# First attention's loop in double steps, second attention's normalisation moved to the end of the key passes

## Chip, cores and metric

The kernel runs on one core of a Trainium2 chip. The metric is the device time of one execution in microseconds (us), as a median over runs: 3865.53 us before the change (3 runs, 3864.57 to 3865.61). A difference of 0.2% is 7.7 us.

## What is computed

Two layers, each an attention, a state-space scan and a feed-forward part, every one added to x. The change touches only the two attentions:

```python
# first attention: one batch entry at a time, 16 entries, 64 queries each, context of 1601 keys
q = (query @ Wq).reshape(b, sq, NUM_HEADS, HEAD_DIM).transpose(0, 2, 1, 3)     # 32 heads of 16
k = (key @ Wk).reshape(b, sk, NUM_KV_HEADS, HEAD_DIM).transpose(0, 2, 1, 3)    # 8 key heads
v = (value @ Wv).reshape(b, sk, NUM_KV_HEADS, HEAD_DIM).transpose(0, 2, 1, 3)
scores = jnp.einsum('bhqd,bhkd->bhqk', q, k) * scale
probs = jax.nn.softmax(scores, axis=-1)
out = jnp.einsum('bhqk,bhkd->bhqd', probs, v) ... @ Wo
# second attention: the same with 16 heads of 96, 4 key heads, over context and latents
```

x has 16 entries of 64 tokens and 512 channels; all is float32.

## The kernel before, in words

Every engine has its own program, written out by hand in the order in which it runs; semaphores tie them together. An instruction that waits holds up all that stands behind it on its engine.

**First attention** (`l0_attention`, the tiles named A_...). A first block makes the queries of all entries and the keys and values of entry 0. Then `all_batches` runs over the 16 entries j, which are called batches. A batch has 26 steps: the 4 key heads of half g = 0 over 13 key tiles k of 128 (the last has 65), then those of g = 1. What TensorE (PE) does in a step:

- `scores` (L1053): 4 matmuls into psE, by the keys Kst and queries Qst, in two row groups of 50 rows at once. psE is held once: the step's exponential on ScalarE (ACT, L1020, into one of 3 tiles probs) must have read it before the next step's scores.
- `maximum` (L754): one unit of the row maxima of the *next* half: a matmul pair into psX, which holds two units. VectorE (DVE) reduces each (L724). A half has 16 units: 0 to 3 over the first 512 keys, 4 to 7 and 8 to 11 over 384 each, 12 to 15 over 321. After the last, three small DVE operations and `max_rows` (L763) turn the maxima into rows, which DVE copies into Qst (L735).
- `weigh` (L1068) of the step *before*: 8 matmul instructions in four column groups (17 columns wide), probs by values, into psO.
- `project` (L785): a third or half of a chunk of the next batch's keys (K, in g = 0) or values (V, in g = 1): 12 passes for each of 4 chunks of 512, 384, 384 and 321 columns, over the full array, into psY. After a V chunk's two steps a third ("T", L774) turns it over with transposes through psY, and ACT copies it out into V (L716, `drain`).

So a step has up to three kinds of PE work, and each kind uses the array in another shape: row groups of 50 (scores, maxima), column groups of 17 (weigh), the full array (project, turns, max_rows).

```python
for u in units[:1]:
    maximum(pe, *to, u)
scores(n)
for u in units[1:]:
    maximum(pe, *to, u)
if n:
    weigh(n - 1)
key, passes = projection(s // 2, s % 2, k)
```

A K chunk goes: PE passes, ACT copy to Kf, GpSimd (POOL) split into high and low parts (L698, L699), then SyncE (SP) writes it to DRAM (L672), waits until that has landed, and reads it back in four pieces in the layout of Kst (L678); the maxima of the next batch's first half are the first to need it. SP does the four chunks one after the other (`stack_k`), and between them saves sums and reciprocals (`save`) and, after the second, loads a chunk of context (`reload`, L664). After the 13 tiles of a half ACT copies psO out (`sums_out`, L1007), and DVE takes one reciprocal of it (L1032, 256 columns), in front of unit 4 of a half.

**Second attention** (`l1_attention`, tiles named D_...): again 16 batches; between the scores and weighing of one batch and the next, PE makes the next batch's keys (L1802, K chunk c, third t), values (L1812) and maxima (L1840) through two psY buffers. DVE copies each third out in two operations, high part (L1756) and low part (L1757), reduces the maxima (L1762), and in `normalise` takes the reciprocal of the denominators (L2149) and multiplies the sums with it (L2152).

Of the kernel before, what the change touches and what calls it, by code (L numbers as in the profile page):

```python
# [12 lines left out]
P = 128  # L13
# [520 lines left out]
def l0_attention(nc, consts, X, x_rows, ctx_in, Wq, Wk, Wv, k_scratch, q_scratch, o_scratch, den_scratch):  # L534
# [17 lines left out]
    NX = NU + 1  # L552
# [4 lines left out]
    K_STEPS = [(0, 3), (3, 3), (6, 3), (9, 3)]  # L557
    PASSES = [(c, a, a2) for c in range(DC) for a, a2 in ((0, 0), (0, 1), (1, 0))]

    def maxima(k):  # L560

        return range(min(NU, NU * k // 10), min(NU, NU * (k + 1) // 10))

    def projection(j, g, k):

        for c in range(NC if j + 1 < B else 0):
            if g == 0:
                first, count = K_STEPS[c]
                if first <= k < first + count:
                    n = len(PASSES) // count  # L570
                    return ("K", j + 1, c), range(n * (k - first), n * (k - first) + n)
            elif k // 3 == c:
                if k % 3 == 2:
                    return ("T", j + 1, c), None
                n = len(PASSES) // 2
                return ("V", j + 1, c), range(n * (k % 3), n * (k % 3) + n)
        return None, None

    with ExitStack() as stack:
# [54 lines left out]
        def step_body(first):  # L634
# [6 lines left out]
            def nth_y(key):  # L641
                kind, b, c = key
                if first:
                    return c if kind == "K" else NC + 2 * c + "VT".index(kind)
                return 3 * NC * (b - 1) + (c if kind == "K" else NC + 2 * c + "VT".index(kind))

            def nth_x(b, g, u):
                return u if first else NX * (2 * b + g - 1) + u

# [68 lines left out]
            def read_maxima(dve, link, b, g, between=None):  # L718
                for u in range(NU):
                    if between and u == 4:  # L720
                        between()
                    x, w = nth_x(b, g, u), CH[u // 4][1]
                    dve.wait_ge(x_full, x + 1)
                    nc.vector.tensor_reduce(mxc[:, u % 4, :, u // 4], psX[:, x % 2, :, 0:w], axis=AX_X, op=ALU.max  # L724
                                            ).then_inc(x_free, 1)
                dve.wait_ge(x_free, nth_x(b, g, NU))
# [4 lines left out]
                x = nth_x(b, g, NU)  # L731
# [6 lines left out]

            def maximum(pe, b, g, u):
                x, c4, pair, qt = nth_x(b, g, u), u // 4, 2 * g + u % 4 // 2, u % 2  # L740
# [17 lines left out]
            def max_rows(pe, b, g):  # L758
                x = nth_x(b, g, NU)
                pe.wait_ge(x_free, x - 1)  # L760
                pe.wait_ge(mp_ready, x // NX + 1)
                for n in range(4):
                    last = nc.tensor.matmul(psX[:, x % 2, 0, bass.ts(n, P)], mpz[:, n, :], identr[:, :],  # L763
                                            start=True, stop=True)
                last.then_inc(x_full, 1)
# [35 lines left out]
            def first_batch():  # L801


                with nc.Block() as block:
# [68 lines left out]
                    def _(dve):  # L873
# [23 lines left out]
                        read_maxima(dve, link, 0, 0)  # L897
# [47 lines left out]
            def all_batches():  # L945
# [3 lines left out]
                with nc.Block() as block:  # L949
                    @block.sync  # L950
                    def _(sp):
# [7 lines left out]
                        def save_reciprocals(s):  # L959
                            sp.wait_ge(inverted, s + 1)  # L960
# [6 lines left out]
                        for j in range(B):  # L967
                            if j > 0:
                                sp.wait_ge(e_full, STEPS * j)
                            if j + 1 < B:  # L970
                                queries(sp, j + 1)
                                for c in range(NC):
# [3 lines left out]
                                    if c == 1 and j > 0:  # L976
                                        reload(sp, NC * j - 1)
# [23 lines left out]
                    def _(act):  # L1001
                        def sums_out(s):
                            act.wait_ge(probs_used, KT * (s + 1))
                            if s >= 2:
                                act.wait_ge(o_out[s % 2], 16 * (s // 2))
                                act.wait_ge(inverted, s - 1)
                            nc.scalar.activation(OT[:, s % 2, :], psO[:, 0:HQ], ACT.Copy).then_inc(o_copied, 1)  # L1007

                        for n in range(N):
                            s, k = divmod(n, KT)  # L1010
                            if k:
                                done, passes = projection(s // 2, s % 2, k - 1)
                                if done and (passes is None or passes[-1] == len(PASSES) - 1):
                                    drain(act, done)
                            if s and k == 1:
                                sums_out(s - 1)
                            if n >= NPR:
# [3 lines left out]
                                                 psE[0:KW[k], :], ACT.Exp, scale=HD ** -0.5).then_inc(e_free, 1)  # L1021
                        sums_out(2 * B - 1)

                    @block.vector
                    def _(dve):
                        link = Chain(dve, dch)

                        def invert(s):
                            dve.wait_ge(o_copied, s + 1)
                            if s >= 2:  # L1030
                                dve.wait_ge(rec_out[s % 2], 16 * (s // 2))
                            nc.vector.reciprocal(RT[:, s % 2, :], OT[:, s % 2, :]).then_inc(inverted, 1)  # L1032

                        nc.vector.memset(psO[:, 0:HQ], 1.0).then_inc(sums_cleared, 1)
                        for s in range(1, 2 * B):
                            read_maxima(dve, link, s // 2, s % 2, (lambda: invert(s - 2)) if s >= 2 else None)
                        for s in range(2 * B - 2, 2 * B):
                            invert(s)

                    @block.tensor  # L1040
                    def _(pe):
                        def scores(n):
# [4 lines left out]
                            if k == 0 and s:  # L1047
                                pe.wait_ge(x_free, nth_x(j, g, NU) + 1)
# [9 lines left out]
                        def weigh(n):  # L1058
# [5 lines left out]
                            for c, (t0, nt) in enumerate(TILES):  # L1064
                                if g == 0 and k == t0 and j:
                                    pe.wait_ge(y_free, nth_y(("T", j, c)) + 1)
# [9 lines left out]
                        for n in range(N):  # L1076
                            s, k = divmod(n, KT)
                            to = divmod(s + 1, 2)
                            units = maxima(k) if to[0] < B else ()
                            for u in units[:1]:  # L1080
# [1898 lines left out]
```

## Time and profile before

| | |
|---|---|
| median of 3 runs | 3865.53 us |
| the profiled execution's own time | 3856.49 us |
| its span | 3854.8 us |
| PE busy | 3619.2 us, 94% |
| DVE busy | 2254.2 us, 58% |
| ACT busy | 1607.5 us, 42% |
| POOL busy | 1281.2 us, 33% |
| first attention's scores, first to last start | 102.6 to 1009.6 us |
| second attention's keys, first to last start | 1397.3 to 3043.4 us |

The terms below are taken against the span of the profiled execution, of which its own time is 1.7 us more; the median is 9.0 us above that time, so a difference found in the span is subtracted from the median. A busy PE is not a PE at its peak, since a matmul's recorded length contains its way through the array: what work costs is read from start to start.

### The profile page before, as it was taken

What the parts mean: (1) busy time and instruction counts of PE and PEld (TensorE: products, weight loads), DVE (VectorE), ACT (ScalarE), POOL (GpSimd) and SP (SyncE); (2) the same over time, 40 slices, a digit from 0 to 9 for tenths busy, and PEclk for the clock granted to TensorE, in tenths of its full rate; (3) what the DMA queues carried; (4) which work ended last, traced back from release to release, by engine and by line L of the source; (5) the groups of instructions that cost most, each with busy time, mean ns of one, the idle gap of its engine ahead of it and who ended that gap; (6) DMA issues with size and microseconds to landing.
All of it is one profiled execution on the core that took longest, in us unless ns stands there. A gap on an engine that the chain in (4) does not pass through costs nothing. (4 is left out here: it accounts for less than half of the span.)

```text
span 3854.8 us, 75904 instructions
## 1 busy us (share of the span) xinstructions
PE 3619.2 (94%) x32856; PEld 2526.8 (66%) x32856; DVE 2254.2 (58%) x2469; ACT 1607.5 (42%) x2213; POOL 1281.2 (33%) x792
## 2 busy tenths in 40 slices
PE   7999999999779779999999999999999998797998
PEld 4555556555345555788888888888888846454554
DVE  4666666666369852555555555555555515697972
ACT  2555555555269421222222222222222103697950
POOL 4344344342048520222222222222221004285861
PEclk8999999999789889999999999999999999898999
DMA  6455555553111032111111111111111112111110
GB/s 209 126 136 148 141 140 147 141 138 103 41 55 52 12 142 80 29 42 41 49 41 49 41 41 50 41 49 41 49 41 45 72 42 55 41 51 31 52 45 22
DMA packets 215252, 277.14 MB, mean 72 GB/s; under 512 B 67056, under 2 KB 165328, under 8 KB 213632
## 3 DMA queue, kind: packets, MB, share of 16 engines
q1 hardware_dynamic: 214920, 272.28, 24.3%
q8 instruction: 261, 4.28, 0.5%
q14 instruction: 71, 0.58, 0.1%
HBM read 218.63 MB, written 53.13 MB: 70 GB/s over the span
## 5 line engine op out<-in xcount | busy, mean ns | idle before, releaser
L1727 POOL TENSOR_TENSOR D_ctx_lo<-D_ctx_raw,D_ctx_hi 128x2048 fp32r<-128x2048 f32 (+1 forms) x64 | 269.7, 4214 | 1217.8 <-ACT D_ctx_hi L1721 1217.8
L724 DVE TENSOR_REDUCE A_mxc<-A_psX 128x2 f32<-128x768 f32 (+2 forms) x512 | 485.4, 984 | 206.1 <-PE A_psX L754 205.2
L1020 ACT ACTIVATE A_probs<-A_psE 128x1024 f32<-128x1024 f32 (+1 forms) x416 | 426.3, 1025 | 317.3 <-PE A_psE L1053 312.0
L1746 ACT ACTIVATE D_V<-D_psY 128x384 f32<-128x384 f32 x208 | 101.9, 490 | 904.3 <-PE D_psY L1812 904.3
L1762 DVE TENSOR_REDUCE D_mxc<-D_psE 128x4 f32<-128x1536 f32 (+2 forms) x128 | 241.9, 1890 | 235.0 <-PE D_psE L1840 235.0
L2103 ACT ACTIVATE D_probs<-D_psE 128x2048 f32<-128x2048 f32 x112 | 210.4, 1879 | 295.6 <-PE D_psE L2216 295.6
L330 POOL TENSOR_TENSOR ES_hcp<-E_du,E_Cn 128x512 f32<-128x512 f32 x224 | 284.8, 1275 | 128.3 <-DVE E_du L357 97.9
L2232 PE MATMUL D_psO<-D_probs,D_V 128*32 128x256 f32 (+1 forms) x5376 | 313.4, 381 | 0.0
L1802 PE MATMUL D_psY<-D_ctx_hi,D_wk_hi 128*128 128x384 f32 (+2 forms) x768 | 279.9, 364 | 13.4 <-DVE D_K_lo L1757 12.7
L1812 PE MATMUL D_psY<-D_wv_hi,D_ctx_hi 128*128 128x384 f32 x832 | 285.3, 343 | 0.0
L1812 PE MATMUL D_psY<-D_wv_hi,D_ctx_lo 128*128 128x384 f32 x832 | 279.0, 335 | 0.0
L1812 PE MATMUL D_psY<-D_wv_lo,D_ctx_hi 128*128 128x384 f32 x832 | 278.5, 335 | 0.0
L357 DVE TENSOR_TENSOR_SCAN E_du<-ES_dA,ES_dB 128x512 f32<-128x512 f32 x224 | 262.4, 1205 | 19.0 <-PE ES_dB L401 12.5
L1802 PE MATMUL D_psY<-D_ctx_hi,D_wk_lo 128*128 128x384 f32 (+2 forms) x768 | 268.3, 349 | 0.0
L1802 PE MATMUL D_psY<-D_ctx_lo,D_wk_hi 128*128 128x384 f32 (+2 forms) x768 | 268.2, 349 | 0.0
L1068 PE MATMUL A_psO<-A_probs,A_V 128*17 128x256 f32 (+1 forms) x3328 | 267.7, 394 | 0.2 <-ACT A_probs L1020 0.2
L2143 DVE TENSOR_TENSOR D_acc<-D_acc,D_probs 128x1024 f32<-128x1024 f32 x96 | 135.8, 1415 | 213.7 <-ACT D_probs L2103 212.1
L2232 PEld LDWEIGHTS D_psO<-D_probs,D_V 128*32 128x32 f32 (+1 forms) x5376 | 163.2, 110 | 115.8 <-issue 9.0
L754 PE MATMUL A_psX<-A_Kst,A_Qst 50*128 50x384 f32 (+2 forms) x1024 | 217.1, 421 | 12.4 <-DVE A_mxc L724 5.9
L417 PE MATMUL ES_acc<-ES_hcp,all_ident 128*128 128x512 f32 x448 | 228.3, 596 | 0.0
L401 PEld LDWEIGHTS ES_dB<-all_ident,ES_scaled 128*128 128x128 f32 x1024 | 128.1, 145 | 133.6 <-issue 80.1
L2211 PE MATMUL D_psE<-D_Q_hi,D_K_hi 32*128 32x256 f32 (+1 forms) x2688 | 207.9, 294 | 5.7 <-PEq L49 5.7
(369 smaller groups left out, 7793.9 us busy)
## 6 DMA issues: line engine op xcount, KB each, us to landing
A_land<-in_ctx SPq DMA_DIRECT2D x32, 768.0 KB, 6.1
D_ctx_raw<-in_ctx SPq DMA_DIRECT2D x32, 768.0 KB, 4.7
A_land<-in_ctx SPq DMA_DIRECT2D x16, 1024.0 KB, 5.7
D_ctx_raw<-in_ctx SPq DMA_DIRECT2D x16, 1024.0 KB, 5.4
E_Cn<-bc_scratch SPq DMA_DIRECT2D x64, 256.0 KB, 3.3
k_scratch<-A_Khl SPq DMA_DIRECT2D x32, 384.0 KB, 5.2
A_Kst<-k_scratch SPq DMA_DIRECT2D x64, 192.0 KB, 3.6
A_land<-in_ctx SPq DMA_DIRECT2D x16, 642.0 KB, 4.4
```

Source lines behind the costliest of these rows:

```text
L330: nc.gpsimd.tensor_tensor(hcp[:, k % NP, :], h_sb[:, k % NP, :], rows.C[:, q % NR, :], ALU.mult).then_inc(hcp_ready, 1)
L357: nc.vector.tensor_tensor_scan(to, decay(s), entering, 0.0, ALU.mult, ALU.add).then_inc(h_ready, 1)
L417: nc.tensor.matmul(acc[:, c, :], consts["ident"][:, :], product, start=(n == 0), stop=(n == N_STATE - 1)).then_inc(summed, 1)
L724: nc.vector.tensor_reduce(mxc[:, u % 4, :, u // 4], psX[:, x % 2, :, 0:w], axis=AX_X, op=ALU.max).then_inc(x_free, 1)
L754: last = nc.tensor.matmul(psX[:, x % 2, o, 0:w], Qst[b % 2][rows, pair, P * qt:P * qt + P], Kst[b % 2][rows, pair, k0:k0 + w], start=True, ...
L1020: nc.scalar.activation(probs[0:KW[k], n % NPR, :, :].rearrange("p h q -> p (h q)"), psE[0:KW[k], :], ACT.Exp, scale=HD ** -0.5).then_inc(e ...
L1068: last = nc.tensor.matmul(psO[32 * h:32 * h + HD + 1, 0:HQ], V[j % 2][0:KW[k], k, HG * g + h, :], probs[0:KW[k], n % NPR, 2 * (h % 2) + h ...
L1727: nc.gpsimd.tensor_tensor(ctx_lo[c][:, :, 0:w], ctx_raw[c][:, :, 0:w], ctx_hi[c][:, :, 0:w].bitcast(F32), ALU.subtract).then_inc(lo_done[c ...
L1762: nc.vector.tensor_reduce(mxc[:, H * a:H * a + H, c], psE[:, :, 0:CH[c][1]], axis=AX_X, op=ALU.max).then_inc(x_free, 1)
L1802: last = nc.tensor.matmul(to[:, 0:w], wk_parts[a][:, d, bass.ts(t, P)], parts[a2][:, d, 0:w], start=(n == 0), stop=(n == len(PASSES) - 1))
L1812: last = nc.tensor.matmul(to[0:KWD[k], 0:H * HD], parts[a][:, d, at], wv_parts[a2][:, d, :], start=(n == 0), stop=(n == len(PASSES) - 1))
L2232: last = nc.tensor.matmul(psO[32 * h:32 * h + 32, t, :], V[0:KWD[k], k, h, bass.ts(t, 32)], probs[0:KWD[k], N % NPR, h, bass.ts(i, NQ)], s ...
```

## The change

In the first attention the 26 steps of a batch become 13 double steps d (0 to 12; `HALVES`, `RUNS`, `UNITS`, `TURNS` are tables by d). In a double step PE does: scores of the even step, up to two maxima, the weighing of the two steps *before*, scores of the odd step, the third maximum, then, all on the full array, the rows of maxima (d = 5 and 12), six or twelve passes of projection, and the turn of a V chunk (d = 8, 10, 12, and 0 of the next batch). At d = 6 the last tile of the first half is weighed by itself right after the next scores, so that d = 7 has one to weigh. The maxima of a half begin at d = 6 (first half of the next batch) and d = 12 (second half), and their rows are turned in the double step behind the last unit. A turned V chunk now goes through psX and is copied by DVE, not through psY and ACT. SP loads the context chunk after all four K chunks. The reciprocal is taken in two halves of 128 columns at d = 1, 2 and 8, 9.

In the second attention DVE's `normalise(j)` moves from behind the first maximum to behind the last K third.

```diff
+    TWOS = STEPS // 2
+    HALVES = (range(6), range(6, 12))
+    RUNS = [("K", 0, HALVES[0]), ("K", 0, HALVES[1]), ("K", 1, HALVES[0]), ("K", 1, HALVES[1]),
+            ("K", 2, range(12)), ("K", 3, range(12)), ("V", 0, HALVES[0]), ("V", 0, HALVES[1]),
+            ("V", 1, HALVES[0]), ("V", 1, HALVES[1]), ("V", 2, HALVES[0]), ("V", 2, HALVES[1]), ("V", 3, range(12))]
+    TURNS = {8: 0, 10: 1, 12: 2, 0: 3}
+    ROWS_FIRST, ROWS_BEHIND = 5, 12
+    UNITS = ((3, 3, 2, 3, 3, 2), (2, 3, 3, 3, 3, 2))
...
+            def values_out(dve, key):
+                b, c = key[1:]
+                x, (t0, nt) = nth_x(key), TILES[c]
+                dve.wait_ge(x_full, x + 1)
+                nc.vector.tensor_copy(V[b % 2][:, t0:t0 + nt, :, 0:HD],
+                                      psX[:, x % 2, 0, 0:P * nt].rearrange("p (j h d) -> p j h d", j=nt, h=H)
+                                      ).then_inc(x_free, 1)
...
                                     stack_k(sp, j + 1, c)
                                     if c == 0 and j > 0:
                                         save(2 * j - 1)
-                                    if c == 1 and j > 0:
-                                        reload(sp, NC * j - 1)
+                                if j > 0:
+                                    reload(sp, NC * j - 1)
...
+                        for j in range(B):
+                            for d in range(TWOS):
+                                exponential(STEPS * j + 2 * d)
+                                exponential(STEPS * j + 2 * d + 1)
+                                key, passes = projection(j, d)
+                                if key and passes[-1] == len(PASSES) - 1:
+                                    drain(act, key)
...
+                        weighed = 0
+                        for j in range(B):
+                            for d in range(TWOS):
+                                n = STEPS * j + 2 * d
+                                behind, ahead = maxima(j, d)
+                                scores(n)
+                                for _, b, g, u in behind:
+                                    maximum(pe, b, g, u)
+                                for e in range(weighed, n):
+                                    weigh(e)
+                                weighed = n
+                                scores(n + 1)
+                                for _, b, g, u in ahead:
+                                    maximum(pe, b, g, u)
+                                if (n + 1) % KT == 0:
+                                    weigh(n)
+                                    weighed = n + 1
+                                if rows_of(j, d):
+                                    max_rows(pe, *rows_of(j, d)[1:])
+                                key, passes = projection(j, d)
+                                if key:
+                                    project(pe, key, passes)
+                                if turned(j, d):
+                                    turn(pe, turned(j, d))
...
                     read_maxima(dve, nxt, 0)
-                    normalise(j)
                     keys_out(dve, link, nxt, 1, 0)
                     keys_out(dve, link, nxt, 1, 1)
...
                         keys_out(dve, link, nxt, c + 1, 2)
+                    normalise(j)
                     read_maxima(dve, nxt, 6)
```

PE in the first attention's loop, before: the end of a project block, one step, and the start of its project block (L785 projects, L754 is a maximum, L1053 scores, L1068 weighs).

```order
L785 MATMUL A_psY<-A_ctx_hi,A_wvlo 128x512
L754 MATMUL A_psX<-A_Kst,A_Qst 128x512 x2
L1053 MATMUL A_psE<-A_Qst,A_Kst 128x256 x4
L754 MATMUL A_psX<-A_Kst,A_Qst 128x512 x2
L1068 MATMUL A_psO<-A_probs,A_V 17x256 x4
L785 MATMUL A_psY<-A_ctx_hi,A_wvhi 128x512
L785 MATMUL A_psY<-A_ctx_lo,A_wvhi 128x512
```

PE at the same loop after the change, double step d = 0 of a batch up to its first passes (L832 projects, L790 is a maximum, L1123 scores, L1138 weighs).

```order
L1123 MATMUL A_psE<-A_Qst,A_Kst 128x256 x4
L790 MATMUL A_psX<-A_Kst,A_Qst 128x512 x4
L1138 MATMUL A_psO<-A_probs,A_V 17x256 x8
L1123 MATMUL A_psE<-A_Qst,A_Kst 128x256 x4
L790 MATMUL A_psX<-A_Kst,A_Qst 128x384 x2
L832 MATMUL A_psY<-A_ctx_hi,A_wkhi 128x512
L832 MATMUL A_psY<-A_ctx_lo,A_wkhi 128x512
```

Two steps' weighing now stands in one block, and one project block follows two scores instead of one.

DVE in the second attention around the first maximum, before (L1756 and L1757 copy a K third, L1762 reduces a maximum, L2149 and L2152 normalise).

```order
L1757 TENSOR_TENSOR D_K_lo<-D_psY,D_K_hi 128x512
L1762 TENSOR_REDUCE D_mxc<-D_psE 128x4
L2149 RECIPROCAL D_recip<-D_psO 128x256
L2152 TENSOR_TENSOR D_OT<-D_psO,D_recip 128x12x64
L1756 CAST D_K_hi<-D_psY 128x384
```

The same engine after the change, at the last K third of a batch (L1835 and L1836 copy, L2228 and L2231 normalise, L1841 reduces).

```order
L1835 CAST D_K_hi<-D_psY 128x385
L1836 TENSOR_TENSOR D_K_lo<-D_psY,D_K_hi 128x385
L2228 RECIPROCAL D_recip<-D_psO 128x256
L2231 TENSOR_TENSOR D_OT<-D_psO,D_recip 128x12x64
L1841 TENSOR_REDUCE D_mxc<-D_psE 128x4 x2
```

The two operations now stand behind all copies of K and in front of the last two maxima.

## Rows read from the trace of the kernel before

**Rows 1.** Engines by stretch, one batch: us, PE, PEld, DVE, ACT, POOL busy, PEclk, DMA, GB/s
```profile
445.00:502.00 57.00, 56.50 (x494) 33.80 (x493) 38.11 (x44) 32.99 (x41) 25.42 (x17) 1.00 0.54 143
```

**Rows 2.** Timeline of PE, first attention: first scores of two batches (start, length)
```profile
446.02 0.49 PE L754 MATMUL A_psX<-A_Kst,A_Qst 50*128 50x512 f32 x2
446.74 0.50 PE L1053 MATMUL A_psE<-A_Qst,A_Kst 50*128 50x256 f32 x4 [0.22 <-ACT A_probs L1020]
...
503.93 0.50 PE L1053 MATMUL A_psE<-A_Qst,A_Kst 50*128 50x256 f32 x4 [0.21 <-ACT A_probs L1020]
```

**Rows 3.** Timeline of PE, one step and the blocks around it
```profile
448.29 0.39 PE L785 MATMUL A_psY<-A_ctx_hi,A_wklo 128*128 128x512 f32 x1
448.52 0.39 PE L785 MATMUL A_psY<-A_ctx_hi,A_wkhi 128*128 128x512 f32 x1
448.84 0.49 PE L754 MATMUL A_psX<-A_Kst,A_Qst 50*128 50x512 f32 x2
449.17 0.39 PE L1053 MATMUL A_psE<-A_Qst,A_Kst 50*128 50x256 f32 x4
449.40 0.39 PE L754 MATMUL A_psX<-A_Kst,A_Qst 50*128 50x512 f32 x2
449.72 0.63 PE L1068 MATMUL A_psO<-A_probs,A_V 128*17 128x256 f32 x8
450.28 0.50 PE L785 MATMUL A_psY<-A_ctx_lo,A_wkhi 128*128 128x512 f32 x1
450.61 0.40 PE L785 MATMUL A_psY<-A_ctx_hi,A_wklo 128*128 128x512 f32 x1
```

**Rows 4.** Timeline of PE, second attention: a weighing of six steps' size in one block
```profile
1900.00 2.80 PE L2232 MATMUL D_psO<-D_probs,D_V 128*32 128x256 f32 x48
1902.62 0.62 PE L2242 MATMUL D_psO<-D_acc,D_ones 128*32 128x256 f32 x8
```

**Rows 5.** Timeline of PE, last batch: two scores with only the exponential between
```profile
980.96 0.50 PE L1053 MATMUL A_psE<-A_Qst,A_Kst 50*128 50x256 f32 x4 [0.48 <-ACT A_probs L1020]
...
982.64 0.50 PE L1053 MATMUL A_psE<-A_Qst,A_Kst 50*128 50x256 f32 x4 [0.62 <-ACT A_probs L1020]
```

**Rows 6.** Timelines of PE and SP: chunk K0 from its last pass to its write
```profile
453.44 0.39 PE L785 MATMUL A_psY<-A_ctx_hi,A_wklo 128*128 128x512 f32 x1
...
456.53 0.38 SPq L672 DMA_DIRECT2D k_scratch<-A_Khl  x1
```

**Rows 7.** Timeline of SP: chunk K2 written and read back, K3 written; landing times of these transfers
```profile
472.14 0.56 SPq L672 DMA_DIRECT2D k_scratch<-A_Khl  x1
478.70 2.46 SPq L678 DMA_DIRECT2D A_Kst<-k_scratch  x4
481.29 0.50 SPq L672 DMA_DIRECT2D k_scratch<-A_Khl  x1
...
DMA to landing us min/median/max: 2.8/3.7/7.4
```

**Rows 8.** Last batch: engines by stretch (columns of rows 1), and timeline of PE in it
```profile
993.00:1000.00 7.00, 6.24 (x44) 2.48 (x40) 0.00 (x0) 3.56 (x4) 0.00 (x0) 0.50 0.00 0
...
993.54 0.80 PE L1053 MATMUL A_psE<-A_Qst,A_Kst 50*128 50x256 f32 x4 [0.19 <-ACT A_probs L1020]
994.27 1.06 PE L1068 MATMUL A_psO<-A_probs,A_V 128*17 128x256 f32 x8
...
995.52 0.80 PE L1053 MATMUL A_psE<-A_Qst,A_Kst 50*128 50x256 f32 x4 [0.19 <-ACT A_probs L1020]
```

**Rows 9.** Timelines of DVE and PE, second attention's key passes
```profile
1839.16 1.76 DVE L1762 TENSOR_REDUCE D_mxc<-D_psE 128x4 f32<-128x1540 f32 x1 [5.84 <-PE D_psE L1840]
...
1906.39 1.75 DVE L2149 RECIPROCAL D_recip<-D_psO 128x256 f32<-128x256 f32 x1
...
1909.05 0.55 DVE L1756 CAST D_K_hi<-D_psY 128x384 fp32r<-128x384 f32 x1
...
1910.24 0.44 PE L1802 MATMUL D_psY<-D_ctx_hi,D_wk_hi 128*128 128x384 f32 x1 [0.85 <-DVE D_K_lo L1757]
```

More of the change, by code:

```diff
@@ new lines, in turned, with rows_of, maxima @@
+    def turned(j, d):
+        b = j if d == 0 else j + 1
+        return ("T", b, TURNS[d]) if d in TURNS and 1 <= b < B else None
+    def rows_of(j, d):
+        if d == ROWS_FIRST:
+            return ("R", j, 1)
+        return ("R", j + 1, 0) if d == ROWS_BEHIND and j + 1 < B else None
+    def maxima(j, d):
+        if d < ROWS_FIRST:
+            b, g, at = j, 1, d + 1
+        elif d < ROWS_BEHIND:
+            b, g, at = j + 1, 0, d - ROWS_FIRST - 1
+        else:
+            b, g, at = j + 1, 1, 0
+        if j == 0 and d < ROWS_FIRST:
+            us = range(NU * d // ROWS_FIRST, NU * (d + 1) // ROWS_FIRST)
+        else:
+            us = range(sum(UNITS[g][:at]), sum(UNITS[g][:at + 1]))
+        units = [("M", b, g, u) for u in us] if b < B else []
+        return units[:2], units[2:]
@@ L579, in l0_attention @@
+    TURN_OF_X = []
+    for j in range(B):
+        for d in range(TWOS):
+            behind, ahead = maxima(j, d)
+            TURN_OF_X += behind + ahead + [key for key in (rows_of(j, d), turned(j, d)) if key]
+    place_x = {key: n for n, key in enumerate(TURN_OF_X)}
     with ExitStack() as stack:
@@ L764, in max_rows, with turn @@
                                             start=True, stop=True)
+                last.then_inc(x_full, 1)
+            def turn(pe, key):
+                b, c4 = key[1:]
+                x = nth_x(key)
+                pe.wait_ge(y_free, nth_y(("V", b, c4)) + 1)
+                pe.wait_ge(x_free, x - 1)
+                for t in range(TILES[c4][1]):
+                    last = nc.tensor.transpose(psX[:, x % 2, 0, bass.ts(t, P)], VT[:, c4 % 2, bass.ts(t, P)],
+                                               consts["ident"][:, :])
                 last.then_inc(x_full, 1)
@@ L1005, in sums_out, with exponential @@
                                 act.wait_ge(o_out[s % 2], 16 * (s // 2))
[L1006 removed]
+                                act.wait_ge(inverted, 2 * s - 2)
                             nc.scalar.activation(OT[:, s % 2, :], psO[:, 0:HQ], ACT.Copy).then_inc(o_copied, 1)
[L1009 removed]
+                        def exponential(n):
                             s, k = divmod(n, KT)
[L1011 to L1014, printed above, removed]
                             if s and k == 1:
```

118 lines of the change are left out of this document (56 added, 62 removed).

## The prediction

> **What bounds the kernel now.** I read the engines by stretch first. In a batch of the first attention PE is busy 56.5 of 57 us at a granted clock of 1.00 (2.4 GHz), DVE 38.1, ACT 33.0, POOL 25.4 [rows 1]: PE sets the end, and the others have room. Then the timeline of PE. The first scores of two batches stand 57.19 us apart (446.74, 503.93) [rows 2]; fifteen batches run like this, the sixteenth has nothing to project. In it PE hardly waits, so the question is what its time is made of, and that is read from start to start inside a step [rows 3]. A projecting pass of 512 columns takes 0.23 us when another follows (448.29 to 448.52), 0.32 when a maximum follows (448.52 to 448.84), and 0.33 as first of its block (450.28 to 450.61). A maximum of 512 columns takes 0.33 behind a pass and 0.32 in front of a weighing, while scores between two maxima take 0.23. So a block on the full array costs 0.19 us more than its passes (0.10 going in, 0.09 going out), and a block of scores and maxima 0.19 too. A weighing takes 0.56 alone (449.72 to 450.28), but 48 instructions of the second attention, six times the size, take 2.62, that is 0.437 each [rows 4]: 0.12 is the price of standing alone.
>
> The same view of the second attention shows one wait per batch: PE stands 0.85 us for a K copy that DVE makes late, because the reciprocal and the multiplication come first [rows 9].
>
> **The change, part by part. Fewer blocks.** A batch had 26 blocks of scores and maxima, 26 weighings and 24 project blocks (12 of K, 8 of V, 4 turns; the rows of maxima join one of these). It gets 26, 14 (one per double step and the extra one at d = 6) and 13. Twelve weighings fewer by 0.12 are 1.44, eleven project blocks fewer by 0.19 are 2.09: 3.53 us a batch, 53.0 over 15. No matmul is added or taken away; transposes and maxima rows only change their place. All of it lies on PE, which has no cover.
>
> **A wait that goes.** At each half's first scores PE stands: a maximum of 512 columns is followed after 0.72 instead of 0.33 (446.02 to 446.74) [rows 2], because that step has nothing to project and the exponential is not ready. Two of 0.39 a batch are 0.78, 11.7 in all.
>
> **Waits that come.** With nothing else between, scores follow scores after 1.68 us, the way through psE and the exponential [rows 5]. From even to odd scores PE now has 0.19 + 0.23 + two maxima (0.46 at 512 columns) + two weighings (0.87 + 0.12) = 1.87; for 384 and 321 columns I estimate the maxima at 0.17 and 0.15, by columns, which leaves 1.75 and 1.71. All are above 1.68, narrowly. At d = 5 there are no maxima: 1.41, a wait of 0.27. At d = 7 one weighing: 1.38, a wait of 0.30. From odd to even there are at least six passes of 384 (1.02) with 0.38 of boundaries and 0.23 of scores, 1.63, and mostly a maximum besides: 0.05 at d = 11. ACT's copy of a finished chunk stands in front of the next exponential; twice a batch I allow 0.1 for it.
>
> DVE takes over four copies of turned values, by the nearest row 0.55 each [rows 9]. They, the halved reciprocals and the reductions fit into its idle 19 us of 57, but the copy holds one of two psX places, and the second maximum of the next double step, some 0.5 later, needs it: I allow 0.12 four times, 0.5. The bounds are 0 and 0.55 each.
>
> **The K chunks on SP.** The first maximum over the last chunk, unit 12, comes six double steps and 0.6 us behind chunk K1's last pass: 6 x 4.2 + 0.6 = 25.8. K1 needs 3.1 to its write (by K0, 453.44 to 456.53) [rows 6]; then SP writes, waits, and issues reads for 2.6 (478.70 to 481.29), for K1, K2 and K3 in turn; K3's last read goes out 2.0 after the first and lands within 3.7 [rows 7]. With a write of 3.7, the median landing, that is 3.1 + 6.3 + 6.3 + 3.7 + 2.0 + 3.7 = 25.1, and nobody waits. K2's write took 6.56 (472.14 to 478.70), with a context load issued just ahead of it, which the change moves behind all four chunks. One such write makes unit 12 late by 2.2, two by 5.0, three by 7.9. I take 0.5, near the median, since what stood ahead of the long one is gone. The moved load itself ends in POOL, which has 31 us to spare a batch.
>
> The added waits are 0.57 + 0.05 + 0.2 + 0.5 + 0.5 = 1.82 a batch, 27.3 in all. A batch goes from 57.19 to 54.70; fifteen give 53.0 + 11.7 - 27.3 = 37.4 us.
>
> **The last batch** has no project block. Its second half runs at 0.50 of the clock (1.2 GHz), after a stretch in which PE waited 0.62 of every 1.68 us [rows 5, 8]. There a step takes 1.98: scores 0.73, a weighing at most 1.06, a wait of 0.19 [rows 8]. In pairs, two weighings stand between even and odd scores (0.73 + 1.06 + about 0.9 = 2.7) and nothing between odd and even (1.98): 4.7 instead of 3.96, +4.7 over 6.5 pairs. At the full clock both would take 1.68, -3.9. The clock was low here before, with the same work, so I take +3 with a small gain in the first half.
>
> **Second attention.** The 0.85 falls away in 15 batches: 12.7 us. `normalise` takes 2.66 (1906.39 to 1909.05) and moves in front of a maximum for which DVE idled 5.84, waiting on PE [rows 9]; if that cover were gone it would delay only maxima 6 and 7, by at most 2.66. The next weighing needs it, far later. Nothing else is late there: the first K copy can start when the first maximum is reduced, 2.66 earlier, against a wait of 0.85.
>
> **Sum.** 37.4 - 3 + 12.7 = 47.1 us. The profiled span goes from 3854.8 to 3807.7, its own time from 3856.5 to 3809.4; the median, 9.0 higher, from 3865.5 to **3818 us**.
>
> **Page against trace.** The rows put 23 fewer blocks at 3.53 us a batch, 0.15 each [rows 3, 4]. The Trainium skill (TensorEngine Tiling (Array Packing), Key Properties) says that changing the tiling mode drains the TensorE, and another page of it (TensorE: Matmul & The Clock Gate, Step-by-step) gives that drain some 128 cycles and lets weight loads be pulled ahead. By these alone a change costs, as an estimate, 53 ns at 2.4 GHz, 23 of them 1.2 us a batch, and the time would be near 3853; the rows show nearly three times that, and I go by them.
>
> **Rivals.** *Only the exit costs.* If of each boundary only the 0.09 going out belongs to the change of shape, and the rest stays with the instructions that wait on semaphores, 23 blocks fewer give 2.07 a batch and not 3.53: 22 us less gain, 3840. Against it: scores wait on a semaphore too and cost nothing extra between maxima. 10%. The draining rule of the Trainium skill named above (TensorEngine Tiling (Array Packing), Key Properties) is this rival read strictly.
>
> *One long write a batch.* Unit 12 is late by 2.2 and not 0.5: 25 us less gain, 3844; 12%.
>
> *The key chunks become the bound, and the kernel is slower.* If two of the three writes take 6.56, PE stands 5.0 us in every batch: 4.5 x 15 = 68 us lost, 3886. The point from which it decides is a wait of 3.6 us (47.1 / 15 on top of 0.5). For it: the chain is serial on SP, the new order leaves it 25.8 us, and landings went up to 7.4 [rows 7]. Against it: the long one had the context load ahead. 5%.
>
> *The moved normalisation changes nothing*, since another copy is late at the same place: 3831; 4%.
>
> **How the numbers follow.** The forecast as summed has 65%; the four rivals 31%; a mixture that ends within 0.2% of before (7.7 us, about what a measurement of this kernel can tell from no change) 4%. Faster by more: 0.65 + 0.10 + 0.12 + 0.04 = 0.91; within: 0.04; slower: 0.05. The range takes, downwards, no wait for K (7.5), none for psX and ACT (10.5), the last batch at full clock (7), and some of the small waits on DVE that I left as they are (6): 3787. Upwards it takes in both rivals at 3840 and 3844 and a little more: 3847.
>
> **What would show it.** Right: first scores of two batches 54.7 us apart; weighings of 16 instructions 0.99 long from start to start; project blocks only once per two scores; no PE wait for D_K_lo. Wrong: PE waiting for scores of d = 0 to 4 (the exponential became the bound), a maximum waiting for a DMA into Kst (the chunks), or pairs of weighings that take 1.1.

## The result, and the profile after

The changed kernel takes **3815.99 us** (median of 4 runs, 3809.24 to 3817.53) against 3865.05 for the kernel before (4 runs, 3860.85 to 3865.61): a ratio of 0.9872, 95% interval 0.9861 to 0.9884, 49.1 us faster. 3818 was forecast, with 3787 to 3847 as range. One run of the kernel with the load back, below, was slow (3915.34 us at a mean granted clock of 0.911, where its nine others have 0.954 to 0.957) and is left out of that kernel's numbers.

The profiled execution of the changed kernel took 3815.09 us, 0.9 under its median; that of before lay 8.6 under its own (9.0 under the median of three runs that the prediction had). So the two spans differ by only 41.4 us where the medians differ by 49.1. The parts below are read from the traces; the sums of medians come from the runs. The head and the busy times of the page after:

```profile
span 3813.4 us, 75996 instructions
PE 3572.9 (94%) x32856; PEld 2539.3 (67%) x32856; DVE 2289.4 (60%) x2561; ACT 1578.1 (41%) x2153; POOL 1281.2 (34%) x792
```

PE's busy share is the same 94% as before, of a span that is shorter. Engines by stretch, first one batch of the first attention (the stretch that answers to [rows 1]), then 30 us of the last batch (columns as in [rows 1]):

```profile
435.47:489.89 54.42, 53.74 (x494) 34.70 (x493) 40.18 (x50) 31.17 (x37) 25.57 (x17) 1.00 0.55 150
950.00:980.00 30.00, 21.94 (x180) 9.31 (x184) 2.86 (x4) 14.81 (x16) 0.00 (x0) 0.61 0.02 6
```

The same 494 matmul records as in [rows 1] now lie in 54.42 us, and PE still has nothing to spare. The timeline of PE, double step d = 0 and the start of its project block, in the columns of [rows 3]:

```profile
489.47 0.49 PE L810 MATMUL A_psX<-all_ident,A_VT 128*128 128x128 f32 x3
489.89 0.50 PE L1123 MATMUL A_psE<-A_Qst,A_Kst 50*128 50x256 f32 x4
490.23 0.88 PE L790 MATMUL A_psX<-A_Kst,A_Qst 50*128 50x512 f32 x4
491.04 1.06 PE L1138 MATMUL A_psO<-A_probs,A_V 128*17 128x256 f32 x16
492.03 0.50 PE L1123 MATMUL A_psE<-A_Qst,A_Kst 50*128 50x256 f32 x4
492.37 0.33 PE L790 MATMUL A_psX<-A_Kst,A_Qst 50*128 50x384 f32 x2
492.63 0.50 PE L832 MATMUL A_psY<-A_ctx_hi,A_wkhi 128*128 128x512 f32 x1
492.97 0.39 PE L832 MATMUL A_psY<-A_ctx_lo,A_wkhi 128*128 128x512 f32 x1
```

Two weighings in one block take 0.99 from start to start (491.04 to 492.03), where two alone took 1.12 [rows 3]. The first pass of a project block still takes 0.34, 0.11 more than one behind another. So the single blocks cost what they did; there are fewer. One row does not fit: two maxima of 512 take 0.81 (490.23 to 491.04) where 0.55 was worked out (0.23 + 0.32). The turn of a V chunk stands just ahead (489.47). The waits of PE and of PE's weight loads (PEld) between 100 and 930 us (us in all, times, longest), those that concern psX:

```profile
PE A_psX L790 <- DMA A_Kst<-k_scratch: 2.7, 4, 1.0
PE A_psX L790 <- DVE A_V L771: 2.6, 15, 0.2
PE A_psX L799 <- DVE A_mxc L748: 2.1, 3, 0.8
...
PEld A_psX L790 <- DVE A_V L771: 19.9, 59, 0.4
```

The last row is the one to see: 59 times, four a batch, the weight load of a maximum waits until DVE has copied a turned V chunk out of psX. With the row of PE itself that is 22.5 us, 1.5 a batch. On PE alone it looks like 2.6, since the load takes the wait. One such wait, at the row that did not fit:

```profile
490.00 0.56 DVE L771 COPY A_V<-A_psX 128x384 f32<-128x384 f32 x1 [0.58 <-PE A_psX L810]
...
490.61 0.19 PEld L790 LDWEIGHTS A_psX<-A_Kst,A_Qst 50*128 50x128 f32 x2 [0.31 <-DVE A_V L771]
```

The copy starts when the turn has left PE (489.47 + 0.49), ends at 490.56, and the second maximum's weights are loaded at 490.61.

In the second attention the timeline of DVE at the last K third of a batch now reads:

```profile
1701.14 0.56 DVE L1836 TENSOR_TENSOR D_K_lo<-D_psY,D_K_hi 128x385 fp32r<-128x385 f32 x1
1701.61 1.75 DVE L2228 RECIPROCAL D_recip<-D_psO 128x256 f32<-128x256 f32 x1
1703.39 0.96 DVE L2231 TENSOR_TENSOR D_OT<-D_psO,D_recip 128x768 f32<-128x768 f32 x1
1707.54 1.76 DVE L1841 TENSOR_REDUCE D_mxc<-D_psE 128x4 f32<-128x1540 f32 x1 [3.19 <-PE D_psE L1919]
```

After both operations DVE still idles 3.19 us for the next maximum, and no wait of PE for D_K_lo, as in [rows 9], is left.

Where the time went, from first scores to first scores in the two traces:

| part | before | after | difference | forecast |
|---|---|---|---|---|
| batches 0 to 14 of the first attention | 858.8 | 824.8 | -34.0 | -37.4 |
| last batch, first to last scores | 47.9 | 48.8 | +0.9 | +3 |
| second attention, first to last scores | 1580.9 | 1567.4 | -13.5 | -12.7 |
| the rest of the span, untouched | | | +5.2 | 0 |

An undisturbed batch takes 54.43 and the mean of batches 1 to 14 is 54.90 (54.70 was forecast, of which 0.5 is the wait for the K chunks); five of these are 0.8 to 2.1 longer than the undisturbed one, by what they wait in two places: 3.8 us in all at unit 12 (from even to odd scores at d = 10) and 2.4 at the rows of maxima (from odd to even scores at d = 12). The +5.2 lies in three untouched stretches (1.6 to 1.8 each). It and the distance between the profiled execution of before and its median belong to this pair of executions, so the terms are settled by timed runs below.

### The profile page after: what moved, and what is told of

It reads as the page before. It is cut to its first block and busy times, and to the rows that moved or that the text cites. A ratio compares the mean times of both kernels' runs of the same rounds, so it can differ in the third digit from the quotient of the medians.

```text
span 3813.4 us, 75996 instructions
## 1 busy us (share of the span) xinstructions
PE 3572.9 (94%) x32856; PEld 2539.3 (67%) x32856; DVE 2289.4 (60%) x2561; ACT 1578.1 (41%) x2153; POOL 1281.2 (34%) x792
## 5 line engine op out<-in xcount | busy, mean ns | idle before, releaser
L1841 DVE TENSOR_REDUCE D_mxc<-D_psE 128x4 f32<-128x1536 f32 (+2 forms) x128 | 241.9, 1890 | 204.2 <-PE D_psE L1919 204.2
L1123 PEld LDWEIGHTS A_psE<-A_Qst,A_Kst 50*128 50x128 f32 (+1 forms) x1664 | 122.9, 184 | 172.1 <-ACT A_probs L1065 116.9
L1123 PE MATMUL A_psE<-A_Qst,A_Kst 50*128 50x256 f32 (+1 forms) x1664 | 211.2, 332 | 27.4 <-ACT A_probs L1065 19.3
L1138 PE MATMUL A_psO<-A_probs,A_V 128*17 128x256 f32 (+1 forms) x3328 | 228.5, 389 | 0.2 <-ACT A_probs L1065 0.2
```

The source lines that it names most:

```text
L1123: last = nc.tensor.matmul(psE[0:KW[k], col:col + HQ], Kst[j % 2][rows, 2 * g + pair, P * k:P * k + KW[k]], Qst[j % 2][rows, 2 * g + pair, ...
L1138: last = nc.tensor.matmul(psO[32 * h:32 * h + HD + 1, 0:HQ], V[j % 2][0:KW[k], k, HG * g + h, :], probs[0:KW[k], n % NPR, 2 * (h % 2) + h ...
L1841: nc.vector.tensor_reduce(mxc[:, H * a:H * a + H, c], psE[:, :, 0:CH[c][1]], axis=AX_X, op=ALU.max).then_inc(x_free, 1)
```

## Experiments

"On the changed kernel" below means against its 3815.99 us. It was timed in one session with the 3865.05 of before, the runs below in two others, in which before took 3862.98 (the first four) and 3862.71 (the last four). Taken against the before of its own session, each of these differences lies some 2 us higher (a gain is smaller by that, a loss larger).

**The second attention alone.** The kernel before, with only `normalise` moved:

```diff
                     read_maxima(dve, nxt, 0)
-                    normalise(j)
...
                         keys_out(dve, link, nxt, c + 1, 2)
+                    normalise(j)
                     read_maxima(dve, nxt, 6)
```

> The kernel before with only the second attention's normalisation moved behind the last K third. Theory (the wait of 0.85 us per batch for the K copy goes, and nothing takes its place): 12.7 us less than before, 15 x 0.85, and no row in which PE waits for D_K_lo. Rival (another copy is late at the same place, or the wait turns up later in the batch): less than 4 us of difference, with a PE wait of some 0.8 us left in each batch.

Measured: 3850.33 us (3844.78 to 3854.98), ratio 0.9967 (0.9954 to 0.998) to the 3862.98 of before in the same session: -12.65. No wait for D_K_lo is left. The term stands, and the rival "changes nothing" falls.

**The first attention alone.** The changed kernel with `normalise` back behind the first maximum:

```diff
                     read_maxima(dve, nxt, 0)
+                    normalise(j)
...
-                    normalise(j)
```

> The changed kernel with the second attention's normalisation put back, so the first attention's part alone. Theory (the parts are independent, and the blocks carry the gain): the first attention's batches stay 54.4 us apart, PE waits 0.85 us per batch in the second attention again, and the time lies 34 us under before (37 for fifteen batches, 3 lost in the last). Rival (the gain of the whole is mostly the second attention or a shift of the later stages): less than 20 us under before.

Measured: 3826.02 us (3822.13 to 3826.27), ratio 0.9907 (0.9891 to 0.9924), -37.0. An undisturbed batch of the first attention stays at 54.42, and the wait for D_K_lo is back, as large as before:

```profile
PE D_psY L1881 <- DVE D_K_lo L1836: 12.7, 15, 0.8
```

The two parts give 12.65 + 37.0 = 49.6 of the 49.1 together: they add.

**What a block boundary costs.** In eight double steps the third maximum goes into the middle of the project block: the same matmuls, one project block and one block of maxima more.

```diff
-                                for _, b, g, u in ahead:
+                                key, passes = projection(j, d)
+                                for _, b, g, u in () if key else ahead:
...
-                                    project(pe, key, passes)
+                                    half = len(passes) // 2
+                                    project(pe, key, passes[:half])
+                                    for _, b, g, u in ahead:
+                                        maximum(pe, b, g, u)
+                                    project(pe, key, passes[half:])
```

> The changed kernel, but in eight double steps of a batch (d = 0 to 3, 6, 7, 9, 10) the third maximum is put into the middle of the project block, not in front of it: the same matmuls, two block boundaries more each (one project block and one block of maxima), and no wait removed or added by semaphores. Theory of the prediction (a block on the full array costs 0.19 us, one of scores or maxima 0.19): the step from odd to even scores grows by 0.38 in these eight, 3.0 us a batch, 46 us in all. Rival 1 (only the exit costs, 0.09): 0.18 each, 1.4 a batch, 22 us. Rival 2 (drain alone, 53 ns a change): 0.11 each, 0.85 a batch, 13 us. Where a maximum comes later, DVE may be late for the next pair at d = 0 and 10; d = 1, 2, 3, 6 and 7 are the clean ones.

Measured: 3854.88 us (3850.74 to 3857.45), ratio 0.9981 (0.9971 to 0.999): +38.9 on the changed kernel. The timeline of PE in it, one such double step:

```profile
627.07 0.50 PE L1123 MATMUL A_psE<-A_Qst,A_Kst 50*128 50x256 f32 x4
627.50 0.50 PE L832 MATMUL A_psY<-A_ctx_hi,A_wkhi 128*128 128x512 f32 x1
627.84 0.39 PE L832 MATMUL A_psY<-A_ctx_lo,A_wkhi 128*128 128x512 f32 x1
628.07 0.39 PE L832 MATMUL A_psY<-A_ctx_hi,A_wklo 128*128 128x512 f32 x1
628.39 0.44 PE L790 MATMUL A_psX<-A_Kst,A_Qst 50*128 50x384 f32 x2
628.76 0.50 PE L832 MATMUL A_psY<-A_ctx_hi,A_wkhi 128*128 128x512 f32 x1
```

The pass in front of the maximum takes 0.32 and the pass behind it 0.34, where 0.23 is one among passes; scores and maximum each pay their exit too. At d = 0 to 3 the time between the two scores grows by 0.39 to 0.40, over all eight by 0.26 to 0.40; the batch goes from 54.43 to 57.41, +2.98. The least growth is at d = 7, which had been named a clean one: there the third maximum took 0.37 in the changed kernel, where 0.26 is usual, and that excess went when it moved. So two blocks cost 0.37 on average, as the boundary rows said. In a batch that much longer PE's waits hold no row for Kst, so the 0.47 by which a mean batch of the changed kernel exceeds its undisturbed one is saved: 15 x (57.41 - 54.90) = 37.7, near the 38.9 timed. (In the two traces the 15 batches differ by 41.0, since batch 0 alone grew by 5.5.)

The experiment prices a block; it does not part the change of the array's shape from the weight load and the semaphore wait that come with it. The trace of the changed kernel speaks for the shape: a pass of 384 columns in front of a turn, on the same full array, takes 0.18 (472.36 to 472.54) where 0.17 is one among passes, and the first pass of 322 behind the rows of maxima, also on the full array, 0.20 (458.59 to 458.79) where 0.15 is usual. That is 0.01 and 0.05, not the 0.09 and 0.11 of a block's edges.

**The turn inside the project block.** Six passes or three, the turn, then the rest, so that passes cover DVE's copy:

```diff
-                                    project(pe, key, passes)
+                                    project(pe, key, passes[:len(passes) // 2])
                                 if turned(j, d):
                                     turn(pe, turned(j, d))
+                                if key:
+                                    project(pe, key, passes[len(passes) // 2:])
```

> The changed kernel, but the turn of a V chunk stands in the middle of the project block of its double step, not behind it. No boundary is added, since both are on the full array. Theory (the second maximum of the next double step waits until DVE has copied the turned values out of psX: the steps from even to odd scores at d = 0, 1, 9 and 11 take 2.14, 2.08, 2.22 and 2.05 where 1.87, 1.75, 1.75 and 1.71 were worked out, 1.4 us a batch): these four steps fall to the worked out values, and the time falls by about 18 us. Rival (the steps behind a turn are long because the transposes leave the array in another state, or because DVE is full there): they stay above 2.0 and the time changes by less than 5 us.

Measured: 3804.44 us (3802.99 to 3812.66), ratio 0.9856 (0.9841 to 0.987), -11.5 on the changed kernel, less than expected. Of the weight loads' waits for A_V one of 0.3 us is left, and the four double steps behind a turn fall to 1.89, 1.77, 1.77 and 1.71, the values worked out before. In the same stretch other waits of PE grew:

```profile
PE A_psX L790 <- DMA A_Kst<-k_scratch: 8.0, 9, 1.8
PE A_psX L799 <- DVE A_mxc L748: 6.8, 10, 1.1
```

Over batches 1 to 14 the double step with unit 12 (d = 10) takes 14.6 us more than when undisturbed (3.8 in the changed kernel), and the stretch with the rows of maxima at d = 12 takes 7.5 more (2.4). The first is the wait for the last K chunk, so time saved ahead of it is waited for there: the key chunks are the next bound. The second, all ten times, follows a DVE operation that lasts as long as one of POOL's (last section). (The profiled execution is the longest of the four, 3810.9 us of span.)

**The context load back between K1 and K2**, as before the change:

```diff
-                                if j > 0:
-                                    reload(sp, NC * j - 1)
+                                    if c == 1 and j > 0:
+                                        reload(sp, NC * j - 1)
```

> The changed kernel, but SP's context load stands again between the second and the third key chunk (as before the change). Theory (this load ahead of K2's write made it take 6.56 us instead of some 4; in the changed kernel it would make the maxima of the last chunk late): the write of K2 takes 6 to 7 us, step 22 of a batch (even to odd scores at d = 11 ... the stretch with unit 12, 1.75 us when nothing waits) grows by 2 to 3 us in most batches, and the time is 25 to 40 us above the changed kernel. Rival (the write is long for another reason, its place beside the other transfers): step 22 stays as it is, time within 8 us of the changed kernel.

Measured: 3867.39 us (nine runs, 3855.19 to 3869.46), ratio 1.0007 (0.9997 to 1.0017): +51.4 on the changed kernel, more than expected; this line alone takes the whole gain away. The timeline of SP shows one K write behind a load, the waits of PE what it costs:

```profile
712.77 0.60 SPq L691 DMA_DIRECT2D A_land<-in_ctx  x1
713.47 0.57 SPq L699 DMA_DIRECT2D k_scratch<-A_Khl  x1
720.05 2.75 SPq L705 DMA_DIRECT2D A_Kst<-k_scratch  x4
```

```profile
PE A_psX L790 <- DMA A_Kst<-k_scratch: 34.1, 23, 2.4
```

From write to read are 6.58 us, as in [rows 7]. In the changed kernel K2 takes 3.91:

```profile
679.65 0.53 SPq L699 DMA_DIRECT2D k_scratch<-A_Khl  x1
683.56 2.46 SPq L705 DMA_DIRECT2D A_Kst<-k_scratch  x4
```

Medians over 13 batches: 6.75 with the load back, 3.99 without. A mean batch has 58.67, 3.77 more than with the load moved; over batches 1 to 14, 52.8. The waits stand at d = 9 and 10, where the units over chunks K2 and K3 are, and not at d = 11, which stays at 2.05.

They are not the whole loss: the row has 34.1 of it. PE behind one of these waits, and the engines by stretch (columns of [rows 1]):

```profile
731.91 0.64 PE L790 MATMUL A_psX<-A_Kst,A_Qst 50*128 50x322 f32 x2 [1.84 <-DMA A_Kst<-k_scratch]
732.48 1.91 PE L1138 MATMUL A_psO<-A_probs,A_V 128*17 128x256 f32 x16
734.32 0.79 PE L1123 MATMUL A_psE<-A_Qst,A_Kst 50*128 50x256 f32 x4
...
732.00:738.00 6.00, 6.00 (x33) 3.83 (x33) 1.66 (x2) 1.02 (x1) 2.31 (x1) 0.50 0.77 230
```

After PE had stood 1.57 us at 726 and 1.84 at 732 for K, its granted clock was 0.50 (1.2 GHz) until 738.6, and two weighings took 1.84 where 0.99 is usual. In batches 1 to 14 such stretches sum to 58.0 us; the changed kernel has none there. The time from odd to even scores at d = 10, in which PE waits for nothing, grew by up to 1.7 a batch, 14.5 in all; half of 58.0 is the most that the clock can have cost. So of the 52.8 us, 14.5 to 29.0 are an estimate of the clock's part: a wait in a loop without slack cost more than its own length.

**Writes ahead of reads.** SP writes the next K chunk before it issues the reads of the one that has landed (K2 before K1's reads, K3 before K2's):

```diff
...
-                                for c in range(NC):
-                                    stack_k(sp, j + 1, c)
-                                    if c == 0 and j > 0:
-                                        save(2 * j - 1)
+                                stack_k(sp, j + 1, 0)
+                                if j > 0:
+                                    save(2 * j - 1)
+                                write_k(sp, j + 1, 1)
+                                for c in range(2, NC):
+                                    write_k(sp, j + 1, c)
+                                    read_k(sp, j + 1, c - 1)
+                                read_k(sp, j + 1, NC - 1)
```

> The changed kernel, but SP writes chunk K2 before it reads K1 back, and K3 before it reads K2 back, each after the write before has landed: the reads no longer stand between the writes. Theory (the chain of writes and reads on SP makes unit 12 late in 6 of 15 batches, by 0.3 to 1.3 us, and the rows of maxima after it): all batches take 54.4 us, no row in which a maximum waits for a DMA into Kst, 6 to 8 us less than the changed kernel. Rival (the long batches come from elsewhere, DVE or POOL): they stay at 55 to 56.5, and the time within 3 us.

Measured: 3809.37 us (3806.5 to 3811.9), ratio 0.9863 (0.9848 to 0.9877), -6.6. Batches 1 to 14 now take 54.41 to 54.70, and of the wait for Kst little remains:

```profile
PE A_psX L800 <- DMA A_Kst<-k_scratch: 0.4, 2, 0.2
```

The intervals of the two kernels' times overlap; that the batches are now alike is the better evidence (0.44 less in the mean, 6.6 in 15). The wait at the rows of maxima is gone here too, and with it the held DVE operation of the last section. The new order moves the context load as well, so this run does not tell which of the two removed it.

**The last half with one weighing per step.**

```diff
-                                if (n + 1) % KT == 0:
+                                if (n + 1) % KT == 0 or (j == B - 1 and d > 6):
...
-                        weigh(N - 2)
```

> The changed kernel, but in the second half of the last batch each step's weighing stands behind the next scores, as before the change, and is not paired. Theory (at 1.2 GHz two weighings between scores take 2.56 where the exponential alone needs 1.98, and nothing fills the other step): the steps there go from 2.56 and 1.98 in turn to 1.98 each, 0.58 less in six pairs, 3.5 us. Rival (the clock follows the idle time, so that another order changes at which clock it runs): steps of 1.68 or of 2.3, a difference of more than 3 us either way from that.

Measured: 3808.71 us (3807.65 to 3812.98), ratio 0.9863 (0.9849 to 0.9878), -7.3. In the trace the last batch falls from 48.8 to 45.9 between first and last scores; the other 4 us are no more than two sets of runs differ by. In both traces the clock falls 27.4 us into the batch, so the rival falls. Timelines of PE in the changed kernel and in this one:

```profile
970.83 0.80 PE L1123 MATMUL A_psE<-A_Qst,A_Kst 50*128 50x256 f32 x4 [1.18 <-ACT A_probs L1065]
971.56 1.91 PE L1138 MATMUL A_psO<-A_probs,A_V 128*17 128x256 f32 x16
973.39 0.79 PE L1123 MATMUL A_psE<-A_Qst,A_Kst 50*128 50x256 f32 x4
975.37 0.80 PE L1123 MATMUL A_psE<-A_Qst,A_Kst 50*128 50x256 f32 x4 [1.18 <-ACT A_probs L1065]
```

```profile
966.35 0.80 PE L1123 MATMUL A_psE<-A_Qst,A_Kst 50*128 50x256 f32 x4 [0.19 <-ACT A_probs L1065]
967.08 1.05 PE L1138 MATMUL A_psO<-A_probs,A_V 128*17 128x256 f32 x8
968.33 0.80 PE L1123 MATMUL A_psE<-A_Qst,A_Kst 50*128 50x256 f32 x4 [0.19 <-ACT A_probs L1065]
```

Scores of 0.80 are those at the lower clock level (1.2 GHz), as in [rows 8]. There, pairs take 2.56 + 1.98 = 4.54, single weighings 1.98 a step, 3.96 for two.

**All three together** (turn inside, writes ahead, last half single).

> The changed kernel with the turns inside the project blocks, the writes of K ahead of the reads, and the last half unpaired. Theory (three waits of different places, each gone as in its own run): batches of 53.0 us (54.43 less 0.25, 0.32, 0.44 and 0.35 of the four steps behind a turn), none longer, the last batch 3.5 shorter: 15 x 1.9 + 3.5 = 32 us less than the changed kernel's mean batch of 54.9 gives, 3784 us. Rival (with the turn's wait gone the key chunks become the bound whatever SP's order): batches of 54 to 55, and less than 15 us.

Measured: **3783.35 us** (3781.6 to 3785.13), ratio 0.9796 (0.9781 to 0.981): 79.4 under before and 32.6 under the changed kernel. Batches 1 to 14 take 53.02 to 53.31. Engines by stretch, one batch, and what is left of the wait for Kst:

```profile
532.12:585.20 53.08, 52.69 (x495) 34.12 (x494) 39.38 (x51) 31.14 (x36) 25.59 (x16) 1.00 0.59 153
```

```profile
PE A_psX L800 <- DMA A_Kst<-k_scratch: 0.2, 1, 0.2
```

The turn's 1.4 a batch now comes through, since the chunks no longer take it back: 15 x (54.90 - 53.09) = 27, and 3 at the end.

## Why the prediction was right

**Fewer blocks (53.0) and the page against the trace.** The price of the project blocks is shown by the third experiment: 0.37 for two blocks on average and 0.39 to 0.40 at d = 0 to 3, where the rows gave 0.38. "Only the exit costs" needed 0.18 and falls. The 1.44 a batch for the weighings rests on rows alone (0.99 for two in one block, 1.12 for two single ones). The Trainium skill (TensorEngine Tiling (Array Packing), Key Properties) has the mode change drain the TensorE; that agrees in kind, but two of the drains priced in the prediction by its other page (TensorE: Matmul & The Clock Gate, Step-by-step) would be 0.11, an estimate. The measurement decides: 0.37 to 0.40.

**Waits that come.** From even to odd scores the working gave 1.87, 1.75 and 1.71; the double steps without a turn ahead have 1.89 (d = 12), 1.75 to 1.78 and 1.71. Behind a turn (d = 0, 1, 9, 11) they take 2.14, 2.08, 2.22 and 2.05. The step that failed is "I allow 0.12 four times, 0.5": it is 0.27 + 0.33 + 0.47 + 0.34 = 1.4 a batch, against bounds of 0 and 2.2. I set DVE's copy of 0.55 against the distance to the second maximum, but the copy starts only when the turn is out of PE, and the maximum's weight load waits with it. Two things gave most of these 0.9 back. The 0.2 for ACT's copies were not needed. And waits of the maxima for DVE's reductions, which the sum had left as they were, went away: up to the last batch PE's weight loads held this row before and hold none after.

```profile
PEld A_psX L754 <- DVE A_mxc L724: 27.6, 112, 0.4
...
485.35 0.19 PEld L754 LDWEIGHTS A_psX<-A_Kst,A_Qst 50*128 50x128 f32 x2 [0.28 <-DVE A_mxc L724]
```

By start-to-start times they cost about 0.5 a batch, an estimate: in the trace of before scores take up to 0.47 (484.88 to 485.35) where 0.23 is usual, while DVE catches up after its reciprocal of 1.74, which the change halves. That the halving did it was not tried by itself. With the turns inside and the writes ahead a batch takes 53.05, where the working without the waits for psX, K and ACT gives 53.50; the difference of 0.45 is of that size. So the undisturbed batch of 54.43 is only 0.23 over the 54.20 that the forecast has without its K term, and the mean of 54.90 is 0.20 over 54.70. That balance was luck.

**K chunks.** 0.5 a batch was allowed for unit 12; the mean batch exceeds the undisturbed one by 0.47, and writing ahead removes 0.44. Only 0.27 of it stands at unit 12, 0.17 at the rows of maxima, so the agreement is in part luck. The 3.7 for a write was a median over writes and reads together; writes alone had 4.2 before, and K1 to K3 took 4.5, 4.0 and 4.0 after. With these the chain is 26.5 long and not 25.1, and unit 12 late by 0.7: "nobody waits" did not hold. That the long write needs the load ahead of it is shown by putting the load back. This one line was worth more than the rival "one long write a batch" gave it (25 us): with it the mean batch is 3.77 longer and the gain is nil, since two chunks come late and the clock falls behind the waits. The rival "the key chunks become the bound" named the right danger.

**Last batch.** +3 forecast, +0.9 in the trace. The pairs at the low clock cost 4.54 (4.7 worked out). Up to the 17th scores the batch gained 2.1; from there it lost 3.0. Of the gain 1.8 was there by the 9th scores, 1.5 of it since the 5th: there PE of before ran 6.8 us (970.5 to 977.3) at the lower clock level and PE after did not. Engines by stretch, before and after (columns of [rows 1]):

```profile
961.40:986.00 24.60, 20.82 (x192) 9.67 (x192) 18.34 (x22) 13.58 (x14) 0.00 (x0) 0.86 0.02 6
929.10:954.00 24.90, 18.32 (x214) 9.54 (x215) 17.19 (x23) 15.15 (x17) 0.00 (x0) 1.00 0.03 6
```

Over the 9th to 14th scores, at the full clock in both, pairs are no slower; then the clock fell two steps later, another 0.3. The mechanism of the loss was right, the gain ahead of it too small, and the +0.9 is one execution's: in the traces of the kernels with this last batch it takes 48.8 to 50.6, as the clock falls 27 to 20 us into it, against 47.9 and 48.5 in the two with that of before.

**Second attention.** 12.7 forecast, 12.65 measured alone (8 to 18 by the interval); the cover for `normalise` (an idle DVE in front of maximum 6) held, with 3.19 us left.

**The sum.** First attention with its last batch: -34.4 forecast, -37.0 in the runs of that part alone (29 to 42 by the interval); second: -12.7 against -12.65. The forecast of 3818 took the profiled execution's 9.0 under its median as a constant; after the change it was 0.9. Own times alone, 3809.4 was forecast and 3815.09 came: the pair of traces hides 5.2 us of gain in stretches that nothing touched. That 3818 came so near to 3816 is in part this and the balances above.

## What to carry to other kernels

On a PE that is always busy, count the blocks of one array shape, and price one by the start-to-start times at its edges; an experiment that adds blocks and no work tests that price. When a loop is shortened, list the serial chains beside it (here write, landing, read on SP) with the time that the new loop leaves them: moving one load out of such a chain decided here whether there was a gain. Read the granted clock behind a new wait as well, since here a wait cost more than its length. And a buffer that a second user borrows is paid where the next owner loads its weights, so look at the waits of the weight loads, not at PE's alone.

## What was not expected of the hardware

A tiny DVE operation can take the length of what POOL (GpSimd) does. In the kernel with the turn inside, `L756` (128x8) has a median of 0.177 us; here it starts 0.13 behind a cast on POOL and ends with it, and the rows of maxima wait on PE:

```profile
644.24 1.47 POOL L716 CAST A_ctx_hi<-A_land 128x1536 fp32r<-128x1536 f32 x1
...
644.37 1.37 DVE L756 TENSOR_TENSOR A_mpz<-A_nm,A_mpz 128x8 fp32r<-128x8 f32 x1
...
646.93 0.66 PE L799 MATMUL A_psX<-all_identr,A_mpz 128*128 128x128 f32 x4 [0.69 <-DVE A_mxc L748]
```

POOL's cast ends at 645.71, DVE's operation at 645.74. The Trainium skill (SBUF — State Buffer, SBUF: two separate sides) describes a port pair that DVE operations with two SBUF inputs share with GpSimd, and that the first to start keeps for its whole instruction; the row agrees, 1.37 instead of 0.177. The ten traces agree too: of 320 executions of this operation 19 last over 0.3 us, each of them begins while a POOL instruction runs and ends 0.02 to 0.03 after it, and none of the other 301 begins while one runs. In the kernel with the turn inside ten are held and the rows of maxima wait ten times (6.8 us), in the changed kernel three and three. No run moved POOL's cast away by itself.
